# The text's total of the sum in an attention kernel, moved from step zero to step one of the next group

## The reference

```
h = layernorm(x)
q = rms_norm(h @ q_w + q_b)                      # 16 heads of 32
k, v         = text rows of the context, projected;  k_img, v_img = image rows, projected
out = softmax(q k_img' / sqrt(32)) v_img + softmax(q k' / sqrt(32)) v     # two softmaxes, added
x = x + tanh(g_xattn) * (out @ o_w + o_b)
h = layernorm(x)
x = x + tanh(g_ffn) * (routed top-2 of 8 experts (h) + shared expert (h))
```

## Time and profile before

| | us |
|---|---|
| median of three runs | 1682.02 |
| the profiled execution | 1686.04 |
| its span on the core | 1684.7 |
| PE busy | 1648.1 (98%) |
| VectorE (DVE) busy | 1184.5 (70%) |
| POOL busy | 929.3 (55%) |
| ScalarE (ACT) busy | 819.6 (49%) |

### The profile page before, as it was taken

How to read it: one execution, slowest core, us unless ns; L and a number is a source line. 1 busy time by engine, 2 the same in 40 slices (tenths; PEclk the granted TensorE clock), 3 DMA queues, 4 the chain that set the end, 5 groups by cost and what they waited for, 6 DMA issues and landing times. The chain is left out here.

```text
span 1684.7 us, 24728 instructions
## 1 busy us (share of the span) xinstructions
PE 1648.1 (98%) x8694; PEld 1115.0 (66%) x8694; DVE 1184.5 (70%) x2188; ACT 819.6 (49%) x1520; POOL 929.3 (55%) x350
## 2 busy tenths in 40 slices
PE   6999999999999999999999999999999999999999
PEld 5888887886455555555555555357777778888777
DVE  6876677667888888888888888686544464434465
ACT  4443332335666666666666666642222455554221
POOL 3221221124777777787888777432614667765642
PEclk9999999999999999999999999999999999999999
DMA  9456857746565655565666655222414577885533
GB/s 334 147 176 186 250 174 195 213 155 202 144 165 143 157 138 154 154 165 161 166 168 168 159 156 149 96 76 68 146 44 171 171 254 266 274 270 187 186 95 100
DMA packets 203139, 285.73 MB, mean 170 GB/s; under 512 B 31348, under 2 KB 128388, under 8 KB 202500
## 3 DMA queue, kind: packets, MB, share of 16 engines
q1 hardware_dynamic: 197464, 267.30, 53.7%
q0 software_dynamic: 5120, 16.78, 3.0%
q10 hardware_dynamic: 432, 0.07, 0.0%
HBM read 206.40 MB, written 110.62 MB: 188 GB/s over the span
## 5 line engine op out<-in xcount | busy, mean ns | idle before, releaser
L1343 ACT ACTIVATE P<-ps 128x512 f32<-128x512 f32 (+1 forms) x832 | 439.2, 600 | 217.8 <-PE ps L1178 216.5
L1449 DVE TENSOR_REDUCE mp<-ps 128x1 f32<-128x448 f32 x720 | 411.9, 616 | 76.4 <-PE ps L1158 73.6
L1560 POOL TENSOR_TENSOR sacc<-sacc,P 128x2048 f32<-128x2048 f32 x90 | 396.4, 4405 | 16.8 <-ACT P L1343 6.0
L1158 PE MATMUL ps<-Kst,Qst 96*128 96x448 f32 x960 | 336.1, 370 | 2.8 <-DVE stl L642 1.7
L1178 PE MATMUL ps<-Qst,Kst 100*128 100x512 f32 (+1 forms) x832 | 322.5, 411 | 4.6 <-ACT P L1343 4.0
L1158 PEld LDWEIGHTS ps<-Kst,Qst 96*128 96x128 f32 x960 | 182.4, 190 | 157.0 <-DVE mp L1449 90.2
L838 POOL TENSOR_TENSOR cl<-craw,ch 128x1024 fp32r<-128x1024 f32 (+2 forms) x26 | 62.0, 2383 | 284.0 <-ACT ch L566 284.0
L1101 PE MATMUL ps<-P,Vg 128*32 128x512 f32 (+2 forms) x1544 | 200.5, 606 | 0.2 <-ACT P L1343 0.2
L1178 PEld LDWEIGHTS ps<-Qst,Kst 100*128 100x128 f32 (+1 forms) x832 | 152.5, 186 | 68.2 <-ACT P L1343 25.6
L49 PE MATMUL ps<-W,ch 128*128 128x512 f32 (+1 forms) x408 | 162.5, 398 | 0.0
L51 PE MATMUL ps<-W,cl 128*128 128x512 f32 (+1 forms) x408 | 159.7, 391 | 0.0
(11 more groups left out here) (264 smaller groups left out, 3125.6 us busy)
## 6 DMA issues: line engine op xcount, KB each, us to landing
gur<-in_w_gate_up SPq DMA_DIRECT2D x23, 1024.0 KB, 7.5
Kst<-KHd SPq DMA_DIRECT2D x56, 320.0 KB, 4.8
Vd<-vf SPq DMA_DIRECT2D x50, 256.0 KB, 2.2
craw<-in_ctxT SPq DMA_DIRECT2D x24, 512.0 KB, 4.5
KHd<-sth SPq DMA_DIRECT2D x24, 512.0 KB, 3.5
KLd<-stl SPq DMA_DIRECT2D x24, 512.0 KB, 4.9
dnr<-in_w_down SPq DMA_DIRECT2D x23, 512.0 KB, 3.8
xg<-Xg SPq DMA_DIRECT2D x23, 512.0 KB, 7.8
```

Source lines behind the costliest of these rows:

```text
L1158: ins = pe.matmul(ps[:, bank, 0:c1 - c0], Qst[G % 3][0:96, j, 128 * qt:128 * qt + 128], Kst[s][0:96, j, c0:c1], start=True, stop=True)
L1343: act.activation(P[slot(G, kt)][:m, j, :], ps[:m, 2 + (e - 1) % 3, :], ACT.Exp, scale=SCALE).then_inc(a_exp, 1)
L1449: dve.reduce_max(out, ps[:, bank:bank + k, 0:cols] if k > 1 else ps[:, bank, 0:cols], AX.X).then_inc(d_ra, 1)
L1560: pool.tensor_tensor(sacc[:, h], sacc[:, h], P[slot(G, kt)][:, h], ALU.add).then_inc(g_sum, 1)
```

## The change

The product with `sacc` becomes a function of its own, `text_total_of_sum`, with its wait. For groups 0 to 14 it is called in `image_total`, in step 1 of the next group, ahead of the image's two totals. For the last group it stays where it was, at the end of `image`.

```diff
+        def text_total_of_sum(G):
+            pe.wait_ge(d_add, 4 * G + (4 if G < NG - 1 else 9))
+            pe_heads(TOTALS, lambda j: ones[:, TEXT if G < NG - 1 else ALL, :], sacc, 0, 128, False, G == NG - 1).then_inc(p_tot, 1)
+
         def image(G):
 
             weigh(G, 11, 0, 128, False, False)
             weigh(G, 12, 0, 65, False, True)
-            pe.wait_ge(d_add, 4 * G + (4 if G < NG - 1 else 9))
-            pe_heads(TOTALS, lambda j: ones[:, TEXT if G < NG - 1 else ALL, :], sacc, 0, 128, False, G == NG - 1).then_inc(p_tot, 1)
+            if G == NG - 1:
+                text_total_of_sum(G)
 
         def image_total(G):
             if G == NG - 1:
                 pe.wait_ge(d_ra, ra)
                 total(G, 10, 64, 128, True, False)
+            else:
+                text_total_of_sum(G)
             total(G, 11, 0, 128, False, False)
             total(G, 12, 0, 65, False, True)
```

## The result

The changed kernel takes 1698.11 us (median of six runs, 1695.84 to 1700.20) against 1681.70 (six runs, 1680.20 to 1683.65). The ratio is 1.0097 with a 95% interval of 1.0086 to 1.0108: 14.5 to 18.2 us slower. A second series, run with the first experiments, gave 1.0093 (1.0077 to 1.0109). The forecast was 1695.3, 0.8% slower. The profiled execution took 1700.20 us, its span is 1698.9 us, 14.2 more than before's.

The account below looks back on a forecast made before the run. PE's written order was taken to bound the kernel, with step zero's first score held by a DMA. 13 x 0.885 + 0.9 + 0.885 = 13.3 us on 1682.0 gave 1695.3 us; range 1689 to 1703.

Parts of the forecast that it names:

- The shadow: Step zero: the sum lies under the first score's wait for the maxima rows' DMA; removing its 0.885 us gains nothing.
- rival D: Tile sacc's waits: 15.3 us idle are PE's and go at 15 of 16 places (1667.7), or only 2.03 goes (1680.0); chance 0.03.
- The price in step one: Step one, ahead of the image's totals: the sum lies in the open and costs 0.885 us at each regular boundary, 11.5 us.
- Nothing is given back: Stretches after step one: none of the delay is recovered over a whole group, so the full 0.885 us a boundary stays.
- The first boundary: First group boundary: the sacc stall of 2.03 us goes, gaining 0.1 to 0.2 us; net cost +0.7 to +1.7, taken 0.9.
- last boundary: Boundary to group 15, no units: first score stays at its DMA, totals become longer, ACT waits for later scores; +0.885 us.
- rival A: PE's clock at group boundaries: low clock at several boundaries, the range's upper end allowing for three; chance 0.07.

Follow-up runs that it names:

- four corners: A product in step zero or not, in step one or not: before, the changed kernel, neither (1.0011 against before) and both (1.0082 against before).
- only_last: Before, with the changed kernel's order at the last boundary alone (group 14 to 15): 1683.96 us, 1.0016 against before.
- after_again: The changed kernel run once more, unaltered, beside runs of before on the same chip: 1695.93 us, 1.0093 against before.
- spare_in_zero: Changed kernel plus a spare product of the same size where the sum stood in step zero, 14 boundaries: 1695.64 us, 1.0090 against before.
- no_sum: Before, with the product with sacc left out altogether for groups 0 to 14, step one as before: 1682.41 us, 1.0011 against before.

## Why the prediction was right

**The shadow.** Right, by trace and by the four corners: the third unit came 0.90 us earlier, the score not at all, and the pause that opened is 0.84 us at the boundary shown (11.4 us over 14, where "some 10 us at 15" was written; the 1.9 us of the first boundary come on top). The 15.3 us of the tile's view were not PE's, so rival D falls too: of them only the 2.0 us at the first boundary went.

**The price in step one.** 0.885 us was taken; measured 0.85 at the regular boundaries (11.0 us over 13 groups) and 0.86 at the bare last one. The pitch from product to product was a little too long a measure. That the sum of the earlier trace rows had waited some hundredths for DVE's addition may be a part of it, which is not shown: in step one, with no such wait, the totals follow the sum after 0.88 us (675.42 - 674.54), and the unit follows them after 1.83 instead of 1.86.

**Nothing is given back.** Right: the 13 groups are longer by 13 times the 0.85 us that the product adds in step one. The 47.25 against 44.25 us in before's own trace had shown this without an experiment.

**The first boundary.** The third unit did start at the bank's release and the score at its DMA (2.43 us behind it), and the stall of 2.03 us for `sacc` vanished. PE of the changed kernel there:

```profile
442.83 0.77 PE L1178 MATMUL ps<-Qst,Kst 100*128 100x512 f32 x1 [1.94 <-issue]
...
447.90 1.85 PE L1101 MATMUL ps<-sacc,ones 128*32 128x512 f32 x8
...
451.40 0.47 PE L1158 MATMUL ps<-Kst,Qst 96*128 96x448 f32 x1
```

From the first values product to the score it takes 5.23 us (442.83 - 437.60) instead of 5.49 (443.37 - 437.88), a gain of 0.26 where 0.1 to 0.2 was forecast. From the score to the unit behind the totals it takes 8.57 us instead of 7.45 (450.82 - 443.37), 1.12 more. Together 0.86; the distance from this group's transposes to the next ones went from 49.43 (485.90 - 436.47) to 50.30 us (486.49 - 436.19), +0.87, and 0.9 was taken.

**The term that was mis-sized** is the last boundary, forecast at 0.885. In the two profiled executions it cost 7.05 - 4.50 = 2.55 us from the first score to the one behind the totals (1085.23 - 1078.18 in the changed kernel). A stretch of low clock fell into the three products:

```profile
1081.01:1084.42 3.41, 3.41 (x20) 0.85 (x16) 0.00 (x0) 1.29 (x3) 0.00 (x0) 0.50 0.79 229
1084.42:1087.83 3.41, 2.77 (x13) 0.86 (x5) 0.94 (x1) 2.06 (x5) 0.00 (x0) 1.00 1.20 463
1087.83:1091.24 3.41, 3.35 (x11) 1.26 (x15) 3.24 (x2) 2.55 (x6) 0.00 (x0) 0.50 0.73 315
```

(stretches of the changed kernel, columns as in rows 1). The last boundary of before's profiled execution has a low stretch too, behind the totals and not in them:

```profile
1074.33:1077.74 3.41, 3.41 (x14) 0.93 (x18) 2.95 (x2) 1.78 (x4) 0.00 (x0) 0.50 1.31 563
```

The prediction, which set the stretch from 1077.74 to 1091.00 us at full clock against rival A, passed over this fall just ahead of it. So the low clock of rival A did come in, at one boundary out of 15, and in two stretches instead of before's one; that the new pause brought it there is not shown. It differs between executions: `only_last`, which has the same order at this boundary, has 5.36 us there and no low clock, `after_again` and `spare_in_zero` 6.57 each. At the 13 regular boundaries the pauses of some 0.8 us brought no fall:

```profile
449.54:1081.00 631.46, 618.44 (x3799) 319.94 (x3795) 533.00 (x985) 408.36 (x782) 489.69 (x154) 1.00 0.58 152
```

So the sum is 11.0 + 0.9 + 2.5 = 14.4 us, against 14.2 between the two spans. The median's 16.4 us holds some 2 more; the second series has 14.9, and the intervals of both (14.5 to 18.2, 12.9 to 18.3) hold 14.4 or touch it. That before's profiled execution lay 4.0 us above its median was taken as common to both kernels; the changed one's lay 2.1 above. Such a distance belongs to the single execution, as the last section shows. Two errors partly cancel in the total, which is luck: the regular boundaries were forecast 0.5 us too high and the last one 1.7 too low.

## What to carry to other kernels

Work that an in-order engine does while it would wait for a transfer is free there, and costs its full length where the engine has no wait: before moving it away from a wait, look at what the next instruction waits for, by its distance from that thing's issue, not by recorded idle time. A cover that fits exactly shows no idle time at all: the profile of before had 0.3 us of this wait, and taking the cover away opened 11.4. "Leave it out" and "put a spare one in", in both places, settle whether a place is free with two or three kernels.

## What was not expected of the hardware

Two profiled executions of the changed kernel differ by 4.3 us (1700.20 and 1695.93), and so do the places where TensorE's clock falls. In the first the first low stretch lies at 442.71 to 449.54 us, in the second (`after_again`) at 396.40 to 403.20:

```profile
442.71:449.54 6.83, 6.71 (x20) 4.20 (x24) 4.13 (x7) 4.07 (x7) 3.90 (x4) 0.50 0.63 141
```

```profile
396.40:403.20 6.80, 6.80 (x18) 5.36 (x18) 5.80 (x11) 5.19 (x9) 0.76 (x1) 0.50 0.50 154
```

The second boundary's transposes start at 486.5 us in the one and at 482.5 in the other:

```profile
L464 PE MATMUL ps<-ident,mx x56: 272/273/273, 482.5 to 1070.0; 128*8 128x128 f32 x56
```

and from there to the last they take 587.5 us in both. Only 3.0 of the 4.0 us are the low stretch's: from the first boundary's score to the unit behind the totals it takes 8.57 us in the one (442.83 to 451.40) and 5.58 in the other (441.80 to 447.38). The other 1.05 us were there before either stretch, since the first score of the attention starts at 396.42 in the one and at 395.37 in the other:

```profile
396.42 0.40 PE L1178 MATMUL ps<-Qst,Kst 100*128 100x512 f32 x1
```

```profile
395.37 0.39 PE L1178 MATMUL ps<-Qst,Kst 100*128 100x512 f32 x1
...
441.80 0.47 PE L1178 MATMUL ps<-Qst,Kst 100*128 100x512 f32 x1 [1.94 <-issue]
```

By the first boundary's transposes the early stretch has cost PE 0.85 us of that lead (436.19 against 435.99). It costs the kernel nothing, for the score there waits for its DMA, which is issued 1.04 us earlier (439.36 against 440.40). Of the 14 profiled executions eight had the low stretch near 396 us and seven one near 443 (`no_sum` had both).

The pause ahead of that score is 1.94 us in both executions, and the clock fell at its end in one alone. So the pause by itself does not say whether the clock falls, and the prediction's comparison of lengths under rival A (a pause of 1 us against the 2.03 us that a fall followed) had less behind it than it seemed. Why an execution gets the early or the late stretch was not tried. A difference of a few us between two profiles of this kernel is therefore read after these stretches and the start of the attention have been compared, or over groups that hold no low stretch.
